# Paired padding writes, twenty first tiles, idle products and moved norm and router places in an attention and expert kernel

## The reference

```
h = layernorm(x)
q = h @ Wq + lora_q(h)                      # 16 heads of 64
k, v of context[:, :73], with lora          # 73 ordinary keys
ki, vi of context[:, 73:]                   # 4 further keys, own weights
a = softmax(q k) v + softmax(q ki) vi
x = x + a @ Wo + bo + lora_o(a)
h2 = layernorm(x)
top 2 of 8 experts by h2 @ gate_w, softmax weights over the two
x = x + sum over the two of weight * (silu(h2 @ w1[e]) @ w2[e])
```

## Time and profile before

| | us |
|---|---|
| median of 3 runs | 741.42 |
| lowest and highest | 741.09, 745.17 |
| the profiled execution | 745.7 |
| its span, first to last instruction | 743.7 |
| PE busy | 674.2 (91%) |
| DVE busy | 548.5 (74%) |
| POOL busy | 495.5 (67%) |
| ACT busy | 455.4 (61%) |

### The profile page before, as it was taken

The page is one execution under the profiler, slowest core; times in us unless marked ns, Lnnn a source line. Parts: engine busy times, 40 slices in busy tenths (PEclk is TensorE's granted clock), DMA queues, the critical chain, the costliest instruction groups (busy, mean ns, idle before and its releaser), DMA issues.

```text
span 743.7 us, 22841 instructions
## 1 busy us (share of the span) xinstructions
PE 674.2 (91%) x7980; PEld 560.0 (75%) x7981; DVE 548.5 (74%) x1239; ACT 455.4 (61%) x768; POOL 495.5 (67%) x582
## 2 busy tenths in 40 slices
PE   6637799999999999999999999779979999999994
PEld 2226688788778878878877887568869888888993
DVE  3953778898898898889889889875737555555552
ACT  1435878778777877877877787544624344434441
POOL 3115546877887887788778788765666656665665
PEclk9997999999999999999999999899989999999998
DMA  9911101211211112121121121133655654454550
GB/s 268 321 48 47 31 21 34 75 33 46 76 38 52 62 45 62 46 74 33 46 76 43 47 63 48 42 99 77 147 132 103 96 91 85 80 90 80 94 79 1
DMA packets 51558, 56.35 MB, mean 76 GB/s; under 512 B 15104, under 2 KB 45824, under 8 KB 51520
## 3 DMA queue, kind: packets, MB, share of 16 engines
q1 hardware_dynamic: 37136, 38.50, 18.1%
q0 software_dynamic: 14384, 17.33, 13.4%
HBM read 30.67 MB, written 25.76 MB: 76 GB/s over the span
## 4 chain that ended last, share of the span: by engine, by line
PE 52%; DVE 17%; issue 10%; SPq 6%; DMA 5%; ACT 5%; POOL 4%; POOLq 1%; DVEq 0%
PE ps L1532 37%; PE ps L1650 5%; DVE pt_s L1268 4%; PE ps L1630 4%; DVE sm L1338 3%; DVE q_s L1268 2%; PE ps L1705 2%; PE ps L529 2%; DVE v_s L1268 2%; POOL out_x L499 2%; DMA out_x<-pt_s,token_of 2%; ACT q_s L1062 1%; DVE x_sb L1363 1%; PE ps L1563 1%; DMA pt_s<-in_wo 1%
## 5 line engine op out<-in xcount | busy, mean ns | idle before, releaser
L499 POOL DMA_INDIRECT out_x<-pt_s,token_of x78 | 124.9, 1601 | 28.4 <-issue 27.2
L588 ACT ACTIVATE q_s<-ps 128x512 f32<-128x512 f32 x78 | 46.5, 596 | 126.9 <-PE ps L1532 123.1
L715 DVE TENSOR_TENSOR wq_s<-q_s,wq_s 128x512 f16<-128x512 f32 x78 | 55.8, 718 | 80.5 <-ACT wq_s L592 65.7
L1532 PE MATMUL ps<-q_s,ffnw 128*128 128x256 f16 x936 | 110.7, 276 | 1.1 <-DVE q_s L697 1.1
L1532 PE MATMUL ps<-ffnw,wq_s 128*128 x936 | 109.1, 273 | 0.1
L894 POOL TENSOR_TENSOR prob<-prob,mx 128x1168 f32<-128x1168 f32 x64 | 77.6, 1234 | 37.8 <-DVE mx L1331 37.8
L1532 PEld LDWEIGHTS ps<-ffnw,wq_s 128*128 128x128 f16 x936 | 89.8, 98 | 14.2 <-issue 2.6
L1532 PEld LDWEIGHTS ps<-q_s,ffnw 128*128 x936 | 91.0, 99 | 12.4 <-issue 1.5
L1532 PE MATMUL ps<-xt_s,wq_s 128*128 128x256 f16 x768 | 90.2, 279 | 1.9 <-DVE xt_s L1268 1.9
L1532 PE MATMUL ps<-wo_s,ot_s 128*128 128x256 f16 x768 | 89.4, 273 | 1.4 <-DVE ot_s L1268 1.4
L1532 PEld LDWEIGHTS ps<-xt_s,wq_s 128*128 128x128 f16 x768 | 76.8, 100 | 13.0 <-issue 1.9
(11 more groups left out here) (210 smaller groups left out, 1230.5 us busy)
## 6 DMA issues: line engine op xcount, KB each, us to landing
prob<-rows_dram SPq DMA_DIRECT2D x39, 264.0 KB
wstage<-in_ffn_w SPq DMA_DIRECT2D x16, 512.0 KB, 3.6
x_sb<-in_x SPq DMA_DIRECT2D x4, 1024.0 KB, 10.7
out_x<-x_sb SPq DMA_DIRECT2D x16, 256.0 KB
rows_dram<-wstage SPq DMA_DIRECT2D x8, 264.0 KB
out_x<-pt_s,token_of POOLq DMA_INDIRECT x78
pt_s<-in_wq SPq DMA_DIRECT2D x2, 512.0 KB, 4.6
pt_s<-in_wo SPq DMA_DIRECT2D x2, 512.0 KB, 8.3
```

The source lines that it names most:

```text
L499: pool.indirect_dma_start(out_rows, bass.IndirectOffsetOnAxis(ap=token_of[:, j % UNROLL, c:c + 1], axis=0), y_sb[:, j % UNROLL, c, :], Non ...
L588: act.activation(h32[:, half, :], h_ps(t, j, half), ACT.Silu, scale=1 / WSCALE).then_inc(silu_done, 1)
L715: dve.tensor_tensor(hs[:, j % 2, 1, 2 * half:2 * half + 2, :].rearrange("p f n -> p (f n)"), h32[:, half, :], hs[:, j % 2, 0, 2 * half:2 * ...
L1532: last = pe.matmul(o, lhs(a, n), rhs(c, n), start=(i == 0), stop=(i == len(steps) - 1))
```

## The change

- `EARLY` becomes 20.
- `fill_up` writes the padding of two experts after each of tiles 3, 7, 11 and 15; the two waits ahead of it stay with the first pair.
- `late_table` is cut in two; its second part, `late_rest`, is called after tile 11.
- In batches 1 to 14, `rstd_2(b - 1)` on POOL goes ahead of `normalise(b, 1)`; on ACT `normalise_2(b - 1)` goes behind `pt(b, 1)` and `x2t_copy(b - 1)` behind `pt(b, 5)`; on PE `transpose_2(b - 1)` goes ahead of `transpose_probs(b, 6)`, with a wait for the second lower half, and `router(b - 1)` ahead of `attend(b, 1)`. In the last batch `normalise_2` goes behind `pt(b, 4)`.
- The value products use the banks 4, 6, 5, 7 in place of 4, 5, 6, 7. The banks of the keys stay as they are.
- `keep_warm` multiplies data that lie in SBUF into bank 0, and nobody reads the result: 12 products of 512 columns after the last batch's new values, 10 after `transpose_2` of batch 14, 6 after the last projection.

```diff
--- before.py
+++ after.py
@@ -58,7 +58,7 @@
 META = 2 * DM
 UNROLL = 4
 CW = ID + ID // 2
-EARLY = 16
+EARLY = 20
 LATE = NT - EARLY
 EARLY_BATCHES = BATCH - 2
 assert (TOPK * EARLY_BATCHES * SEQ - EXPERTS * (RT - 1) + RT - 1) // RT >= EARLY
@@ -388,7 +388,7 @@
 
         def heads_bank(k):
 
-            return ps[:, 4 + k, :]
+            return ps[:, (4, 6, 5, 7)[k], :]
 
         x_bank, out_bank = (ps[:, n, :] for n in (4, 5))
 
@@ -453,11 +453,13 @@
 
             def fill_up(t):
 
-                if t != UNROLL - 1:
+                if t < UNROLL - 1 or t >= 5 * UNROLL - 1:
                     return
-                sp.wait_ge(pad_made, 5)
-                sp.wait_ge(tab_done, 2)
-                for e in range(EXPERTS):
+                if t == UNROLL - 1:
+                    sp.wait_ge(pad_made, 5)
+                    sp.wait_ge(tab_done, 2)
+                pair = (t - UNROLL + 1) // UNROLL * 2
+                for e in (pair, pair + 1):
                     r = sp.value_load(pads[0:1, e:e + 1], min_val=0, max_val=EXPERTS * REGION - RT)
                     sp.dma_start(rows_dram[bass.ds(r, RT), :].rearrange("(c p) n -> p c n", p=P), pad_rows
                                  ).then_inc(pad_in, 16)
@@ -673,6 +675,9 @@
                 dve.tensor_reduce(e_of_all[:, EARLY:NT], past_late, AX, ALU.add)
                 link(spread(flags, delta, LATE))
                 link(dve.tensor_reduce(all_row_of[:, 0:LATE], past_n_late, AX, ALU.add))
+
+            def late_rest():
+                flags = (past_late, past_n_late)
                 link(dve.scalar_tensor_tensor(out=all_row_of[:, 0:LATE], in0=tnum[:, 0:LATE], scalar=float(RT),
                                               in1=all_row_of[:, 0:LATE], op0=ALU.mult, op1=ALU.add))
                 dve.tensor_copy(table_all[:, :, 0:EARLY], table[:])
@@ -685,7 +690,7 @@
                 dve.tensor_copy(adds_all[:, 0:EARLY], adds_early[:])
                 adds(adds_all[:, EARLY:NT], EARLY, LATE, all_starts[:, 0:LATE]).then_inc(tab_done, 1)
 
-            return full_tiles, early_table, all_rows, late_table
+            return full_tiles, early_table, all_rows, late_table, late_rest
 
         def ffn_dve(dve, then, late_table):
 
@@ -962,10 +967,11 @@
                 normalise(b, 0)
                 if routed and not last:
                     scatter(b - 2, 0)
+                if not first and not last:
+                    rstd_2(b - 1)
                 normalise(b, 1)
-                if not first:
+                if last:
                     rstd_2(b - 1)
-                if last:
                     scatter(b - 2, 0)
                 if routed and not last:
                     scatter(b - 2, 1)
@@ -1166,6 +1172,8 @@
                     act.wait_ge(pt_zeroed, 1)
                 pt(b, 0)
                 pt(b, 1)
+                if not first and not last:
+                    normalise_2(b - 1)
                 pt(b, 2)
                 pt(b, 3)
                 if not last:
@@ -1173,14 +1181,14 @@
                     k_(b + 1, 1)
                     put_kipa(b + 1)
                 pt(b, 4)
+                if last:
+                    normalise_2(b - 1)
                 pt(b, 5)
-                if not first:
-                    normalise_2(b - 1)
+                if not first and not last:
+                    x2t_copy(b - 1)
                 pt(b, 6)
                 pt(b, 7)
                 ot(b, 0)
-                if not first and not last:
-                    x2t_copy(b - 1)
                 ot(b, 1)
                 if not first and not last:
                     row_high(b - 1)
@@ -1426,7 +1434,7 @@
                                       picked[:].rearrange("p k t e -> p (k t) e"), AX, ALU.add).then_inc(slots, 1)
                 assert c.n == ROUTE, c.n
 
-            full_tiles, early_table, all_rows, late_table = tile_tables(dve)
+            full_tiles, early_table, all_rows, late_table, late_rest = tile_tables(dve)
 
             def body(b, first, last):
                 routed = not (isinstance(b, int) and b < 2)
@@ -1517,6 +1525,8 @@
                     all_rows()
                 if t == 7:
                     late_table()
+                if t == 11:
+                    late_rest()
 
             ffn_dve(dve, then, lambda: None)
 
@@ -1721,6 +1731,11 @@
                                          stop=(t + pick == TPB + TOPK - 2))
                 last.then_inc(rank_mm, 1)
 
+            def keep_warm(bank, count):
+
+                for i in range(count):
+                    pe.matmul(ps[:, bank, :], wq_s[:, 0, 0, 0:P], wq_s[:, 0, 1, 0:512], start=True, stop=True)
+
             def body(b, first, last):
                 scores(b, 0)
                 if not last:
@@ -1745,6 +1760,8 @@
                 if first:
                     pe.wait_ge(w_split, 3)
                 new_values(b)
+                if last:
+                    keep_warm(0, 12)
                 if not first:
                     pe.wait_ge(x1_done, b)
                 transpose_probs(b, 0)
@@ -1766,6 +1783,9 @@
                 transpose_probs(b, 4)
                 pe.wait_ge(pt_split, 8 * b + 1)
                 transpose_probs(b, 5)
+                if not first and not last:
+                    pe.wait_ge(pt_split, 8 * b + 2)
+                    transpose_2(b - 1)
                 pe.wait_ge(pt_split, 8 * b + 3)
                 transpose_probs(b, 6)
                 if not last:
@@ -1777,8 +1797,6 @@
                 for k in range(4):
                     pe.wait_ge(pt_split, 8 * b + 5 + k)
                     if k == 1 and not first and not last:
-                        transpose_2(b - 1)
-                    if k == 2 and not first and not last:
                         pe.wait_ge(k_split, 2 * b + 4)
                         router(b - 1)
                     attend(b, k)
@@ -1789,10 +1807,12 @@
                 body(b, False, False)
             body(BATCH - 1, False, True)
             transpose_2(BATCH - 2)
+            keep_warm(0, 10)
             project(BATCH - 1, 0)
             pe.wait_ge(slots, BATCH - 1)
             router(BATCH - 2)
             project(BATCH - 1, 1)
+            keep_warm(0, 6)
 
             def then(t):
                 if t == -1:
```

## The result

The kernel after has a median of 736.55 us (734.99 to 739.76, 13 runs). In the same rounds the kernel before had 745.17 (741.09 to 748.19). The ratio is 0.9908, 95% interval 0.9888 to 0.9927: 0.92% faster, which is 6.9 us of 745.17. The two medians lie further apart, 8.6 us; where this text says "by timed runs", it means the ratio. The forecast was 6.8 less, 734.6, in a range of 729 to 740.5. The profiled execution took 735.7 with a span of 733.8; before it was 745.7 and 743.7. That the two profiles lie 9.9 apart while the runs lie 6.9 apart is a first question.

The account below looks back on a forecast made before the run. TensorE, busy 19 to 20 of 20 us through most batches and expert tiles, was taken as the bound. Hole −6.3, tile 20 +0.3, batches −1.0, idle products +0.2 sum to −6.8: 734.6 us, range 729 to 740.5.

Parts of the forecast that it names:

- The hole at 540 us: Before tile 8, TensorE idles 4.03 us behind eight padding writes and the clock falls; pairs gain 6.3 us, bounds 5.5 and 6.9.
- The sum: Whole kernel: −6.3 + 0.3 − 1.0 + 0.2 = −6.8 us, from a median of 741.42 to 734.6.
- +0.3 for tile 20: Expert tiles: tile 20's load must wait until all padding has landed; 0.3 us lost, bounds 0 and 0.8.
- rival D: Expert tiles: the padding stall is cut up, not removed, 2.9 us or more come back; 737.5 to 740 us, chance 0.15.
- Twenty first tiles: Expert tiles: larger tables and the late table in two parts cost nothing, bounds −0.3 and +0.3 us.
- A middle batch: Batches, 14 times: moved work fills 1.4 us of waits, GpSimd delays transposes 4 by 1.24; 0.07 each, 1.0 us gained.
- Rival B: Batches gain 0.3 to 0.6 us each because GpSimd's 1.24 us find slack; about 729.3 us, chance 0.15.
- Rival C: Batches: GpSimd's 1.24 us before transposes 4 carry through; 744.3 us if half stays, 753 if all, chance 0.13.
- Idle products: Last batch to first tile: 28 products mostly fit TensorE's idle time; 0.2 us lost, bounds 0 and 3.5.

Follow-up runs that it names:

- the run in fours: The changed kernel with the padding writes in two groups of four, after tiles 3 and 7; ratio 0.9913 to the kernel before, expert part 236.93 us.
- the experts' part alone: The kernel before with only padding in pairs, twenty first tiles, the late table in two parts and the last batch's normalise_2 moved; ratio 0.9958.
- the batches alone: The kernel before with only the moved places in the batches and the new banks of the value products; ratio 0.9981, 14 batches 366.05 us.
- the old order beside after: The changed kernel with norm, x2 copy, x2 transposes, router and banks in the batches back in their old places; ratio 0.9936, median 738.77 us.
- with the row copy: The changed kernel with the first scatter behind normalise(b, 1) and ScalarE's row copy behind its fourth head copy; ratio 0.9816, median 729.82 us.

## Why the prediction was right, point by point

**The hole at 540 us.** Right in place and cause. SP's row of eight writes is the cause: with them together the hole is there (five profiles, 3.26 to 4.70 us idle before tile 8), in fours and pairs it isn't, with the same number of bytes. The run with all padding at once has the twenty first tiles and the hole, so these don't close it. The sum had −6.3 for the hole and +0.3 for tile 20, −6.0 together. I correct the experts' part of each profile for a low clock in tile 0 (what its first 24 products took over 2.79). The five with all padding at once then give 240.6 to 243.0, mean 241.8; the eight with pairs give 236.0 to 237.5, mean 236.7. That is **−5.1**, 0.9 less than priced. A second cut, at the first transposes of tile 9, says where the 0.9 are:

| from, to | all at once, 5 profiles | pairs, 8 profiles | difference |
|---|---|---|---|
| first product of tile 0 (corrected) to transposes of tile 9 | 50.2 to 52.3, mean 51.4 | 44.8 to 45.7, mean 45.1 | −6.3 |
| from there to transposes of tile 38 | 166.1 to 166.7, mean 166.4 | 167.0 to 168.6, mean 167.7 | +1.2 |

The hole itself gave what was priced: 6.3 in the mean, and 6.8 between the two first profiles (51.8 and 45.0), since the profile of before had one of the larger holes and the idle 0.2 to 0.7 us forecast at tile 8 didn't come. Behind it the tiles 9 to 37 take 1.2 us longer when the padding is spread, where 0.3 was taken for tile 20's load. That load is never waited for; PE loses the time in short gaps of 0.1 to 0.5 us between its products, which the profile lists as "issue", that is, with nothing waited for; one of them in after:

```profile
621.24 2.81 PE L1542 MATMUL ps<-ffnw,wq_s 128*128 x24 [0.33 <-issue]
```

The run with all padding at once lies with the first group (166.4), though all the rest of it is as in after, and the run in fours with the second (167.6). So the loss comes with the spread and not with the twenty tiles; what makes the gaps isn't shown. This decides rival D, too: its stall at the loads didn't come, but about a fifth of the gain was lost behind it. By timed runs the whole is smaller still, 0.48% or 3.6 us between the two ratios, each of which is uncertain by about 2 us, and 0.42% or 3.1 us in the run with the experts' part alone.

**Twenty first tiles.** Not tried apart. The forecast of nothing stands unrefuted: PE has no idle row at the tiles where the tables are made, and the one profile with twenty tiles and all padding at once (240.8) lies among the four with sixteen (240.6 to 243.0).

**A middle batch.** The mechanism came as written. The norm ahead of the normalisation puts transposes 4 later by 1.26 us, measured from the batch's own first scores (376.53 − 356.48 = 20.05 after, 378.16 − 359.37 = 18.79 before), and 1.24 was forecast. From there to the next scores 6.3 was forecast and 6.16 measured. The projection is late next, by 0.15. The size: 14 batches gained 1.9 us between profiles without ACT's lateness (368.0 to 366.1, three profiles with the old order and three with the new: before again, experts alone, idle products alone against after, its repetition and the batches alone), where 1.0 was taken. The reading of the earlier trace rows held one thing that was no property of the kernel: the router's wait of 0.23 and part of the 7.73. In the second profile of before that stretch takes 7.46:

```profile
381.06 1.58 PE L1640 MATMUL ps<-ident,prob 128*77 128x128 f32 x12 [0.15 <-POOL prob L901]
...
388.52 1.04 PE L1630 MATMUL ps<-k_s,q_s 64*128 64x77 f16 x48
```

The gain of such a batch is thus 7.46 − 6.16 = 1.30 less POOL's 1.2, about 0.1. Over the batches 2 to 14 it is 26.29 − 26.20 = 0.09 each, close to the 0.07 forecast, and 1.2 us in all. The rest, 0.7, is batch 1: it goes from 26.20 to 25.47 in these profiles, since it has no scatter on POOL and its transposes 4 pay nothing for the norm. The prediction priced all 14 alike, and that is what was mis-sized in this term. The batch without a scatter also told, before any further run, where more was to be had. By timed runs the 1.9 can't be told from nothing: the old order beside after and the batches alone give 0.1% and 0.2%, with intervals of 0.3% to either side. Rival B, 0.3 or more a batch, would have been read from the two first profiles (26.50 − 26.16 = 0.34); only the repeated profile shows that 0.21 of it was there before by chance. Rival C didn't come, since the transposes' delay was met by as long a stretch of waits.

**Idle products.** Priced at 0.2 lost. From batch 15's first scores to tile 0's first product the nine profiles with them have 36.1 to 37.8, mean 36.8, the five without 36.2 to 37.5, mean 37.0. The difference of 0.2 is less than the spread of either: no cost and no gain is shown there. What they may buy is at tile 0: three of the five profiles without them have a low clock in its first 24 products (5.29, 4.69 and 3.92 us), one of nine with them (4.46). That would be worth about a microsecond as a mean, but both timed comparisons show none (0.9927 beside 0.9926, and 0.9998), with intervals of 0.3% to either side. It stays open. The forecast that the clock "perhaps stays up" over the last batch held in some profiles and not in others (below).

**The sum.** −5.1 − 1.9 − 0.2 = −7.2 by profiles, −6.9 by timed runs, −6.8 forecast. The experts' term was off by 0.9 one way (the 1.2 behind the hole), the batches' by 0.9 and the idle products' by 0.4 the other, and they cancelled. The places and their signs were right by reasoning, but that the sum comes within some tenths is luck, all the more as the ratio's own interval is 1.5 us to either side. Of the 9.9 us between the two first profiles, 2.9 are ACT's lateness in the profile of before (370.94 − 368.04). The predicted 734.6 rests on a median of 3 runs, 741.42; over 13 runs that kernel has 745.17, 3.8 more. The measured 736.55 is only 2.0 above the forecast, since the two medians lie 8.6 apart and not 6.9: 3.8 from the base, less 1.8 by which the medians' distance exceeds the forecast's 6.8. So the level, too, came out closer than its parts.

## What to carry to other kernels

Look at how long a queue that issues loads is held by a run of other issues, and compare that with the slack of the next load: eight writes of 1.2 us in front of one load cost 5 to 7 us by the profiles, four cost 0.4, with as many bytes in all. Count the rest of the stretch as well: spread out, the same writes cost 1.2 us elsewhere. When moving work ahead on one engine fills waits on another, look for what stands in the same queue with nobody waiting for it: here moving the two scatters of 2.7 us was worth over 4 us in 13 batches, more than twice what the norm's move gave, and with the row copy 8. Behind the wait that goes, look for those that it hid: of 1.1 us a batch 0.8 came back. Before a small wait that repeats in a loop is counted, see whether a second profile of the same program has it, and before a gain is multiplied by the number of turns, see which turns lack one of the two sides.

## What the runs showed of the hardware that I had not expected

**A lateness of one execution, repeated in each turn of a loop.** ACT in the profile of before, middle batch, and in the second profile of the same program; the value product that it copies starts at 434.12 in the first and 436.51 in the second:

```profile
435.35 0.60 ACT L1062 ACTIVATE ot_s<-ps 128x512 f16<-128x512 f32 x1 [0.43 <-PE ps L1650]
```

```profile
437.40 0.60 ACT L1062 ACTIVATE ot_s<-ps 128x512 f16<-128x512 f32 x1
```

From the product's start to the copy's are 1.23 us in the first and 0.89 in the second. The batches 1 and 14, which ACT runs outside its hardware loop of twelve turns, have 0.88 and 0.89 in the first profile too. So one place in the loop's code was late in every turn, by 0.30 to 0.39 us, in this execution only; the other profiles with the old order have 0.89 there in every turn. What makes it late no row shows.

**The clock of the same kernel falls in one execution and not in the next.** The profile of after, windows of 1 us in the last batch:

```profile
476.00:477.00 1.00, 0.48 (x3) 0.51 (x4) 0.96 (x3) 0.22 (x1) 0.37 (x2) 0.85 0.00 0
477.00:478.00 1.00, 1.00 (x7) 1.00 (x6) 1.00 (x3) 0.50 (x1) 0.75 (x1) 0.50 0.00 0
```

PE had made 12 idle products (2.76 us) and then waited 2.00. Its repetition had the same products and a wait of 1.98, and the clock stood at 1.00 over the same batch. The fall cost next to nothing in after: its 32 transposes took 5.38 us in one row, while those of the repetition took 1.94 and 1.94 with a wait of 1.35 for POOL between them, 5.23 from start to end. From 466 to 500 us the mean clock is 1.00 in four of the nine profiles with idle products and 0.90 to 0.95 in the other five; in the five without them it is 0.87 to 0.90. Whether a stall costs clock, and whether the lower clock costs time, can thus not be told from one profile.

**DVE's small product beside POOL's large one.** `picked` (128x32) takes 0.18 us in the expert part. In a batch of before it takes 2.13 (390.68 to 392.81) and in after 1.84 (387.78 to 389.62). POOL's pair of subtractions starts at 390.60 and ends at 393.02 in the one, and lasts from 387.40 to 389.83 in the other: `picked` ends 0.21 before the pair in both, however early it came. Seen by single instructions, POOL's pair is one of 2.16 us and a short one behind it:

```profile
390.60 2.16 POOL L894 TENSOR_TENSOR prob<-prob,mx 128x1168 f32<-128x1168 f32 x1
```

`picked` ends 0.05 after the end of the long one, in each of the 14 batches of both profiles in which the two meet. The length of such a row reads POOL's work, not DVE's. This agrees with the rule of the Trainium skill, page "SBUF — State Buffer", section "Who interferes with whom", that the two engines share a pair of ports as an exclusive lock.
